# A state-space layer with a mixture layer on one core: one product of each chunk moved from GpSimd to VectorE, and the accumulation of the step sizes moved from a DMA to GpSimd

## The chip, the core and the metric

The kernel runs on one core of a Trainium2 chip. The engines are TensorE (PE), VectorE (DVE), ScalarE (ACT), GpSimd (POOL) and SyncE (SP), which here only issues DMAs. The metric is the device time of one execution in microseconds; smaller is better.

## What is computed

A block of a sequence model on `u` of shape (4, 2048, 256), in float32: a layer norm, a selective state-space layer with residual, a second layer norm, and a mixture of four experts (top 2, with low-rank additions) with residual. The first half, cut to what the change touches:

```python
x, z = jnp.split(u @ W_in.T + b_in, 2, axis=-1)          # 512 channels each
dbc = x @ W_x.T + b_x                                    # 16 + 16 + 16 columns
delta = softplus(dbc[..., :16] @ W_dt.T + b_dt)
def step(h, xs):                                         # over the time steps, h: (B, 512, 16)
    dt_t, x_t, Bt, Ct = xs
    h = h * exp(dt_t[..., None] * A) + x_t[..., None] * (dt_t[..., None] * Bt[:, None, :])
    y_t = einsum('bdn,bn->bd', h, Ct)
    return h, y_t
```

## The kernel before

The input is cut into 16 chunks of 512 time steps, four batches in turn. Partitions hold channels, the free axis holds time. A chunk's recurrence is worked in 16 steps (`s`, lines 1415 and 1486); step `s = 4 m + k` holds channel block `m` (128 channels) and a group `k` of four of the 16 states, spread over 128 partitions as 32 channels x 4 states in four sub-blocks `j`. For each step:

- POOL multiplies the replicated `delta * x` by the replicated B (`times_b`, L1470, 128x2048): the input of the recurrence, in one of four buffers `hs`, one step ahead of the scans. It may only write `hs` when PE has summed the step four before.
- ACT computes the four decays, `exp(dt * a)` (L1203), into four PSUM banks `decay`.
- DVE runs four scans (L1395, 128x512), one for each `j`, with a decay and an input each.
- The states are multiplied by C in two halves of two `j` (128x1024): `h = 0` always on DVE (`times_c` in DVE's part, L1382, from PSUM to `hs`), `h = 1` on POOL for the steps in `POOL_STEPS` and on DVE for the others. For a step of POOL the scans of `j = 2, 3` write to `hs` instead of PSUM, and POOL multiplies in place (L1482). For a step of DVE they write to PSUM, and the product is issued after the first scan of the next step.
- ACT copies the last column to the state of the batch (`keep_state`, L1217), which frees a pair of decay banks for the next step; PE adds the states up (`sum_states`, L998).

`POOL_STEPS` holds the steps with `k < 3`, 12 of 16.

Everything else of the chunk and its neighbours is laid between these steps by hand-written tables, one for each engine (`PE_SIDE`, `ACT_SIDE`, and so on; other tables for the last chunks). A row is a step. "pre" is work for the next chunk, "main" for this one, "post" and "late" for the ones before. The rows that matter here are of POOL (L111): V1 in step 3 and U1 in step 4, for the channel blocks 2 and 3 of this chunk; V0 in step 11 and U0 in step 12, for blocks 0 and 1 of the next; O1 and O2 (Newton steps of the two layer norms, four tiny instructions each) in steps 1 and 7; W0 in step 13. In a step POOL first issues `times_b` of the next step, then `times_c` of the step before, then the side jobs.

V and U make `delta`. The softplus is computed as `relu(v) + log(1 + exp(-|v|))`. ACT leaves `relu(v)` in `z_dt` and the logarithm in `e_dt` (two channel blocks, 128x1024 each). V adds them: a DMA from `z_dt` to `e_dt` that accumulates, issued from POOL (L1460). U waits for it and writes `delta * x` to `z_dt` (L1450, POOL). SP then stores both to HBM (`store_rep`, L755) and reads them back replicated over partitions into `dt_rep` and `dx_rep` (`load_rep`, L722). For the first two channel blocks of the first chunk DVE does both itself (`first_step`, L1398); so there are 31 V and 31 U.

Of the kernel before, what the change touches and what calls it, by code (L numbers as in the profile page):

```python
# [21 lines left out]
ALU = mybir.AluOpType  # L22
# [13 lines left out]
KG = NS // 4  # L36
STEPS = M * KG
# [309 lines left out]
    "",  # L347
]
BANKS = 3
POOL_STEPS = [s for s in range(STEPS) if s % KG < 3]  # L350
V_PAIRS = [(s, h) for s in range(STEPS) for h in range(2) if h == 0 or s not in POOL_STEPS]
BANK_JOBS = "ABCDEFGHIJTK"
LAST_H = 9
# [4 lines left out]
def split_table(table):  # L358
# [17 lines left out]
             pool=[[[x for x in part if x not in ("O1 pre", "V0 pre", "U0 pre")] for part in row] for row in SIDE["pool"]])  # L376
# [111 lines left out]
def block_program(nc, u, w_in, b_in, w_x, b_x, w_dt, b_dt, a_log, d_skip, w_out, b_out, w_ga, b_g, w_i, w_o,  # L488
                  lora_b, ident_in, nsum_in, tri_in, out):
    with ExitStack() as ctx:  # L490
# [3 lines left out]
        def sem(name):  # L494
            return ctx.enter_context(nc.semaphore(name))
# [34 lines left out]
        z_dt = sb("z_dt", [P, 2, T])  # L530
        e_dt = sb("e_dt", [P, 2, T])
# [73 lines left out]
            "xr_loaded", "ln2_part", "ln2_root", "ln2_newton", "x2_ready", "router", "router_exp",  # L605
            "r1_ready", "z2_ready"))
        sp_turn, dve_turn, last_sums = sem("sp_turn"), sem("dve_turn"), sem("last_sums")
        pool_turn, delta_added = sem("pool_turn"), sem("delta_added")
        skip_ready, bound_ready = sem("skip_ready"), sem("bound_ready")
        mask_step, second_step, weight_step = sem("mask_step"), sem("second_step"), sem("weight_step")  # L610
        weights_ready = sem("weights_ready")
# [10 lines left out]
        def pool_products(c, s):  # L622

            return len(POOL_STEPS) * c + POOL_STEPS.index(s) + 1
        out_stored = [sem(f"out_stored{t}") for t in range(TT)]
# [85 lines left out]
        def _(sp):  # L711
# [20 lines left out]
            def waits(*needs):  # L732


                for s_, at in needs:
                    at_least(sp, s_, at)
                    if not isinstance(at, int):
                        sp.sem_inc(sp_turn, 1)
# [9 lines left out]
            def store_rep(c, pair):  # L748


                back = [(loaded[i], 128 * c - (64 if pair == 0 else 0)) for loaded in (dt_loaded, dx_loaded) for i in range(2)]
                waits(*back, (dx_ready, 2 * c + pair + 1))
                for i in (1, 0) if isinstance(c, int) and c == 0 and pair == 0 else range(2):
                    for kind, src in ((1, z_dt), (0, e_dt)):
                        sp.dma_start(rep_dram[kind, 2 * pair + i], src[:, i, :]).then_inc(rep_stored[2 * pair + i], 16)  # L755
# [11 lines left out]
            def body(c, par, parts):  # L767
# [4 lines left out]
                def multiplied(at, s):  # L772

                    if s in POOL_STEPS:
                        return (prod_vector, vector_products(at, s, 0)), (prod_pool, pool_products(at, s))
# [62 lines left out]
        def _(pe):  # L838
# [148 lines left out]
            def sum_states(c, s, odd):  # L987

                m, k = divmod(s, KG)
                if k == 0:  # L990
                    at_least(pe, gated_ready, M * c + m)
                if s in POOL_STEPS:
                    pe.wait_ge(prod_vector, vector_products(c, s, 0))
# [449 lines left out]
        def _(pool):  # L1443

            def job_pool(letter, i, when, job, c, par):
                q, odd = chunk_of(c, when), odd_of(par, when)
                g = nc.gpsimd
                if letter == "U":
                    pool.wait_ge(delta_added, 16 * (2 * q + i))
                    g.tensor_tensor(z_dt[:], e_dt[:], x_t[odd][:, 2 * i:2 * i + 2, :], ALU.mult).then_inc(dx_ready, 1)  # L1450
                elif letter == "O":
                    newton(pool, g, i, q)
                elif letter == "W":
                    pool.wait_ge(second_step, q + 1)
                    g.tensor_tensor(wgt[odd][:, 1], pexp[:, :, NE], wgt[odd][:, 0], ALU.mult).then_inc(weights_ready, 1)
                elif letter == "V":

                    pool.wait_ge(log_dt, 2 * q + i + 1)
                    pool.sem_inc(pool_turn, 1)
                    g.dma_start(e_dt[:], z_dt[:], accum_op=ALU.add).then_inc(delta_added, 16)  # L1460

            def times_b(c, par, s):

# [95 lines left out]
```

## Time and profile before

| | us |
|---|---|
| median of 3 runs | 1874.48 |
| lowest and highest | 1869.98, 1906.22 |
| the profiled execution | 1869.98 |
| its span | 1868.2 |
| mean granted TensorE clock in it | 0.950 |

The span is the time from the first to the last instruction of the profiled execution. The page's first part gives the busy time of each engine, its second the busy share in 40 slices, in which DVE and POOL stand at nine tenths or more from the second slice to the 37th. An engine's busy share is no proof that it paces the others; the waits between engines have to be read beside it. A row of a timeline gives start, duration, engine, line, operation and tiles, and in brackets the idle time before it with what ended it.

### The profile page before, as it was taken

What the parts mean: (1) busy time and instruction counts of PE and PEld (TensorE: products, weight loads), DVE (VectorE), ACT (ScalarE), POOL (GpSimd) and SP (SyncE); (2) the same over time, 40 slices, a digit from 0 to 9 for tenths busy, and PEclk for the clock granted to TensorE, in tenths of its full rate; (3) what the DMA queues carried; (4) which work ended last, traced back from release to release, by engine and by line L of the source; (5) the groups of instructions that cost most, each with busy time, mean ns of one, the idle gap of its engine ahead of it and who ended that gap; (6) DMA issues with size and microseconds to landing.
All of it is one profiled execution on the core that took longest, in us unless ns stands there. A gap on an engine that the chain in (4) does not pass through costs nothing.

```text
span 1868.2 us, 26288 instructions
## 1 busy us (share of the span) xinstructions
PE 1641.5 (88%) x7052; PEld 834.3 (45%) x7052; DVE 1765.0 (94%) x2060; ACT 1505.7 (81%) x3113; POOL 1717.0 (92%) x649
## 2 busy tenths in 40 slices
PE   6646689998998999899899989989998998998999
PEld 3213244444444444444444444444444544444465
DVE  5999999999999999999999999999999999999941
ACT  4776789788888978888897888889788898977743
POOL 1999999999999999999999999999999999999810
PEclk9767889999999999999999999999999999999999
DMA  6565566656647565654756565575656657565100
GB/s 209 137 142 142 109 153 141 163 119 143 151 99 172 132 170 120 148 142 104 174 129 168 126 144 143 105 173 132 163 128 142 144 105 175 120 160 133 42 18 17
DMA packets 150070, 249.07 MB, mean 133 GB/s; under 512 B 22432, under 2 KB 47264, under 8 KB 149408
## 3 DMA queue, kind: packets, MB, share of 16 engines
q1 hardware_dynamic: 145456, 231.09, 51.2%
q0 software_dynamic: 4464, 16.25, 4.5%
q8 instruction: 61, 1.00, 0.2%
q14 instruction: 89, 0.73, 0.1%
HBM read 188.01 MB, written 42.99 MB: 124 GB/s over the span
## 4 chain that ended last, share of the span: by engine, by line
PE 38%; DVE 30%; issue 13%; ACT 8%; POOL 5%; DMA 2%; SPq 1%; DVEq 0%; ACTq 0%; POOLq 0%
DVE decay L1395 13%; DVE hs L1382 8%; PE bank L914 7%; DVE hs L1395 5%; PE y_ps L998 5%; PE bank L962 5%; PE bank L984 4%; PE bank L936 4%; POOL hs L1470 3%; PE bank L918 3%; ACT decay L1203 2%; POOL hs L1482 2%; PE y_ps L1002 2%; PE bank L908 1%; PE bank L979 1%
## 5 line engine op out<-in xcount | busy, mean ns | idle before, releaser
L1470 POOL TENSOR_TENSOR hs<-dx_rep,b_rep 128x2048 f32<-128x2048 f32 x255 | 1180.6, 4643 | 43.6 <-DVE hs L1411 39.7
L1395 DVE TENSOR_TENSOR_SCAN decay<-decay,state,hs 128x512 f32<-128x512 f32 x640 | 798.7, 1288 | 6.3 <-ACT decay L1203 5.2
L1203 ACT ACTIVATE decay<-dt_rep,a_sb 128x512 f32<-128x512 f32 x1024 | 696.2, 686 | 20.6 <-DVE dx_rep L1409 1.8
L1395 DVE TENSOR_TENSOR_SCAN hs<-decay,state,hs 128x512 f32<-128x512 f32 x384 | 491.5, 1280 | 3.9 <-ACT decay L1203 3.8
L1482 POOL TENSOR_TENSOR hs<-hs,c_rep 128x1024 f32<-128x1024 f32 x192 | 469.3, 2444 | 5.3 <-ACT state L1217 4.6
L1382 DVE TENSOR_TENSOR hs<-decay,c_rep 128x1024 f32<-128x1024 f32 x320 | 389.0, 1216 | 0.0
L998 PE MATMUL y_ps<-hs,nsum 128*32 128x512 f32 x2048 | 291.6, 643 | 61.4 <-POOL hs L1482 40.4
L962 PE MATMUL bank<-w_i_sb,x_t 128*128 128x512 f32 x488 | 259.9, 658 | 5.4 <-DVE silu L1282 5.1
L914 PE MATMUL bank<-xn_t,w_in_sb 128*128 128x512 f32 x512 | 249.8, 616 | 12.2 <-DVE silu L1282 4.3
L984 PE MATMUL bank<-w_o_sb,r_t 128*128 128x256 f32 x944 | 221.0, 388 | 10.3 <-ACT r L1181 6.2
L984 PEld LDWEIGHTS bank<-w_o_sb,r_t 128*128 128x128 f32 x944 | 177.6, 192 | 65.0 <-ACT r L1181 18.2
L1217 ACT COPY state<-decay 128x2 f32<-128x2 f32 x320 | 50.4, 157 | 159.8 <-DVE hs L1382 156.7
L914 PEld LDWEIGHTS bank<-xn_t,w_in_sb 128*128 128x128 f32 x512 | 91.7, 194 | 125.7 <-issue 98.3
L979 PE MATMUL bank<-ident,r 128*128 128x128 f32 x928 | 121.7, 277 | 17.2 <-DVE x L1298 14.3
L962 PEld LDWEIGHTS bank<-w_i_sb,x_t 128*128 128x128 f32 x488 | 89.1, 200 | 104.3 <-issue 86.3
L979 PEld LDWEIGHTS bank<-ident,r 128*128 128x128 f32 x928 | 101.8, 140 | 75.6 <-issue 42.7
L998 PEld LDWEIGHTS y_ps<-hs,nsum 128*32 128x32 f32 x2048 | 41.8, 110 | 172.5 <-issue 150.0
L936 PE MATMUL bank<-w_out_sb,gated 128*128 128x256 f32 x480 | 114.0, 380 | 0.1
L1181 ACT ACTIVATE r<-bank,wgt 128x512 f32<-128x512 f32 x122 | 82.3, 675 | 33.0 <-PE bank L885 33.0
L936 PEld LDWEIGHTS bank<-w_out_sb,gated 128*128 128x128 f32 x480 | 91.6, 191 | 13.2 <-DVE gated L1287 0.5
L885 PE MATMUL bank<-lora_st,low_t 64*128 64x512 f32 x122 | 61.0, 500 | 41.1 <-ACT r L1177 40.8
L1177 ACT ACTIVATE r<-bank,wgt 128x512 f32<-128x512 f32 x122 | 82.8, 678 | 15.5 <-PE bank L966 12.2
(182 smaller groups left out, 1853.8 us busy)
## 6 DMA issues: line engine op xcount, KB each, us to landing
dx_rep<-rep_scratch SPq DMA_DIRECT2D x252, 256.0 KB, 4.7
dt_rep<-rep_scratch SPq DMA_DIRECT2D x252, 256.0 KB, 7.6
b_rep<-bc_scratch SPq DMA_DIRECT2D x256, 64.0 KB, 4.0
c_rep<-bc_scratch SPq DMA_DIRECT2D x256, 64.0 KB, 2.4
rep_scratch<-z_dt SPq DMA_DIRECT2D x64, 256.0 KB, 2.6
rep_scratch<-e_dt SPq DMA_DIRECT2D x64, 256.0 KB, 2.8
e_dt<-z_dt POOLq DMA_DIRECT2D x31, 512.0 KB, 4.9
xin<-in_u SPq DMA_DIRECT2D x16, 512.0 KB, 4.0
```

Of the source, the lines that this page charges most:

```text
L914: mm = pe.matmul(ps[:], w_in_sb[:, k, col:col + P], xn_t[odd][:, k, :], start=k == 0, stop=k == KD - 1)
L936: pe.matmul(ps[:, cols], gated[odd][:, k, i * P:(i + 1) * P], w_out_sb[:, k, :], start=k == 0 and is_last(q) and i % 2 == 0, stop=False, s ...
L962: pe.matmul(ps[:], x2_t[odd][:, k, t * P:(t + 1) * P], w_i_sb[:, k, cols], start=k == 0, stop=False, skip_group_check=is_last(q))
L979: mm = pe.matmul(ps[:, f * P:(f + 1) * P], r[i % 2][:, f * P:(f + 1) * P], ident[:], start=r is r1, stop=r is r2, is_transpose=True)
L984: mm = pe.matmul(ps[:, 0:D], r_t[:, f, :], w_o_sb[:, f, :], start=f == 0, stop=f == NF - 1)
L998: mm = pe.matmul(y_ps[32 * j:32 * j + 32, :], nsum[:], hs[s % 4][:, j, :], start=k == 0, stop=k == KG - 1, skip_group_check=True)
L1177: nc.scalar.activation(r1[i % 2][:], ps[:], ACT.Relu, scale=wgt[odd][:, 0, i // 2:i // 2 + 1]).then_inc(r1_ready, 1)
L1203: nc.scalar.activation(decay[:, j, :], dt_rep[m % 2][:, j, :], ACT.Exp, scale=a_sb[:, J * s + j:J * s + j + 1]).then_inc(decay_ready, 1)
L1382: v.tensor_tensor(hs[s % 4][:, js, :], decay[:, js, :], c_rep[:, k, :].unsqueeze(1).to_broadcast([P, 2, T]), ALU.mult).then_inc(prod_vecto ...
L1395: v.tensor_tensor_scan(hs[s % 4][:, j, :] if kept else decay[:, j, :], decay[:, j, :], hs[s % 4][:, j, :], state[:, b, n:n + 1], ALU.mult, ...
L1470: nc.gpsimd.tensor_tensor(hs[s % 4][:], dx_rep[m % 2][:], b_rep[:, k, :].unsqueeze(1).to_broadcast([P, J, T]), ALU.mult).then_inc(input_re ...
L1482: nc.gpsimd.tensor_tensor(hs[s % 4][:, 2:4, :], hs[s % 4][:, 2:4, :], c_rep[:, k, :].unsqueeze(1).to_broadcast([P, 2, T]), ALU.mult).then_ ...
```

## The change

Two edits that belong together.

1. V becomes a POOL instruction: `e_dt = e_dt + z_dt`, 128x1024, on POOL. It signals on `delta_ready`, which the first step on DVE used already; U waits for that, and so does `store_rep` on SP, beside its old wait for `dx_ready`. Two semaphores and the `sem_inc` ahead of the DMA go. V's and U's places in the tables stay.
2. `POOL_STEPS` loses step 14 (`m = 3, k = 2`). The second half of its product with C goes to DVE, between the first and the second scan of step 15; its scans of `j = 2, 3` write to PSUM. PE then waits for DVE's product alone in that step, ACT copies that state from PSUM, and all counts of products follow from the lists.

```diff
-POOL_STEPS = [s for s in range(STEPS) if s % KG < 3]
+POOL_STEPS = [s for s in range(STEPS) if s % KG < 3 and s != 14]
@@
-        pool_turn, delta_added = sem("pool_turn"), sem("delta_added")
@@ store_rep
-                waits(*back, (dx_ready, 2 * c + pair + 1))
+                waits(*back, (delta_ready, 2 * c + pair + 1), (dx_ready, 2 * c + pair + 1))
@@ job_pool
                 if letter == "U":
-                    pool.wait_ge(delta_added, 16 * (2 * q + i))
+                    pool.wait_ge(delta_ready, 2 * q + i + 1)
@@
                 elif letter == "V":
 
                     pool.wait_ge(log_dt, 2 * q + i + 1)
-                    pool.sem_inc(pool_turn, 1)
-                    g.dma_start(e_dt[:], z_dt[:], accum_op=ALU.add).then_inc(delta_added, 16)
+                    g.tensor_tensor(e_dt[:], e_dt[:], z_dt[:], ALU.add).then_inc(delta_ready, 1)
```

## Rows read from the trace of the kernel before

**Rows 1.** The page's first part: busy time, share of the span, instructions, by engine.
```profile
PE 1641.5 (88%) x7052; PEld 834.3 (45%) x7052; DVE 1765.0 (94%) x2060; ACT 1505.7 (81%) x3113; POOL 1717.0 (92%) x649
```

**Rows 2.** Busy time in a steady stretch, and DVE's once-a-chunk wait, first and last.
```profile
403.80:1606.70 1202.90, 1102.06 (x4812) 565.21 (x4811) 1194.65 (x1378) 1034.14 (x2150) 1188.93 (x453) 0.98 0.60 141
...
420.84 1.28 DVE L1395 TENSOR_TENSOR_SCAN hs<-decay,state,hs 128x512 f32<-128x512 f32 x1 [0.21 <-ACT decay L1203]
...
1513.59 1.28 DVE L1395 TENSOR_TENSOR_SCAN hs<-decay,state,hs 128x512 f32<-128x512 f32 x1 [0.21 <-ACT decay L1203]
```

**Rows 3.** Waits of DVE and POOL in that stretch: us in total, times, longest.
```profile
DVE lg L1325 <- PE bank L946: 4.9, 6, 0.9
POOL z_dt L1450 <- DMA e_dt<-z_dt: 4.4, 10, 0.9
DVE hs L1395 <- ACT decay L1203: 2.5, 11, 0.4
POOL hs L1470 <- PE y_ps L998: 1.7, 5, 1.0
POOL hs L1482 <- ACT state L1217: 0.9, 4, 0.2
DVE decay L1395 <- issue: 0.8, 1, 0.8
```

**Rows 4.** Timeline of DVE, steps 15 and 0 of two chunks.
```profile
685.46 3.64 DVE L1395 TENSOR_TENSOR_SCAN decay<-decay,state,hs 128x512 f32<-128x512 f32 x3
...
692.47 1.23 DVE L1382 TENSOR_TENSOR hs<-decay,c_rep 128x1024 f32<-128x1024 f32 x1
693.59 1.30 DVE L1395 TENSOR_TENSOR_SCAN decay<-decay,state,hs 128x512 f32<-128x512 f32 x1
694.78 1.28 DVE L1395 TENSOR_TENSOR_SCAN hs<-decay,state,hs 128x512 f32<-128x512 f32 x1
```

**Rows 5.** Timeline of POOL around V0 and U0, and a later U1.
```profile
660.61 2.38 POOL L1482 TENSOR_TENSOR hs<-hs,c_rep 128x1024 f32<-128x1024 f32 x1
662.91 0.83 POOL L1460 DMA_DIRECT2D e_dt<-z_dt  x1
663.52 4.80 POOL L1470 TENSOR_TENSOR hs<-dx_rep,b_rep 128x2048 f32<-128x2048 f32 x1
668.03 2.60 POOL L1450 TENSOR_TENSOR z_dt<-e_dt,x_t 128x1024 f32<-128x1024 f32 x1
670.35 4.78 POOL L1470 TENSOR_TENSOR hs<-dx_rep,b_rep 128x2048 f32<-128x2048 f32 x1
...
722.82 2.38 POOL L1450 TENSOR_TENSOR z_dt<-e_dt,x_t 128x1024 f32<-128x1024 f32 x1 [0.41 <-DMA e_dt<-z_dt]
```

**Rows 6.** Timeline of ACT at the same place as rows 4.
```profile
693.73 0.16 ACT L1217 COPY state<-decay 128x2 f32<-128x2 f32 x1 [0.44 <-DVE hs L1382]
693.92 0.69 ACT L1203 ACTIVATE decay<-dt_rep,a_sb 128x512 f32<-128x512 f32 x1
```

**Rows 7.** Timelines of POOL (inputs of steps 9, 10) and DVE (steps 9 and 13).
```profile
637.98 9.04 POOL L1470 TENSOR_TENSOR hs<-dx_rep,b_rep 128x2048 f32<-128x2048 f32 x2
646.97 2.37 POOL L1482 TENSOR_TENSOR hs<-hs,c_rep 128x1024 f32<-128x1024 f32 x1
...
643.67 2.44 DVE L1395 TENSOR_TENSOR_SCAN decay<-decay,state,hs 128x512 f32<-128x512 f32 x2
...
672.13 2.48 DVE L1395 TENSOR_TENSOR_SCAN decay<-decay,state,hs 128x512 f32<-128x512 f32 x2
```

**Rows 8.** Timeline of PE: the sum of step 8.
```profile
651.15 1.06 PE L998 MATMUL y_ps<-hs,nsum 128*32 128x512 f32 x8
```

**Rows 9.** Timelines of POOL and DVE where the second chunk begins.
```profile
140.00 5.03 POOL L1470 TENSOR_TENSOR hs<-dx_rep,b_rep 128x2048 f32<-128x2048 f32 x1
...
143.74 2.61 DVE L1395 TENSOR_TENSOR_SCAN decay<-decay,state,hs 128x512 f32<-128x512 f32 x2
```

**Rows 10.** The page's DMA issues: KB each, median us to landing.
```profile
dx_rep<-rep_scratch SPq DMA_DIRECT2D x252, 256.0 KB, 4.7
...
e_dt<-z_dt POOLq DMA_DIRECT2D x31, 512.0 KB, 4.9
```

**Rows 11.** Timelines of SP and POOL: the reload after U1, and its first use.
```profile
728.16 1.77 SPq L722 DMA_DIRECT2D dx_rep<-rep_scratch  x4
...
738.78 4.53 POOL L1470 TENSOR_TENSOR hs<-dx_rep,b_rep 128x2048 f32<-128x2048 f32 x1
```

## Prediction

> **What bounds the kernel now.** The page's first part comes first [rows 1]: DVE is busy for 94% of the span and POOL for 92%, PE for 88%, ACT for 81%. Two engines are close to full, so the average does not say which one paces. I then asked for the busy times of the steady stretch, eleven chunks long [rows 2]: DVE 1194.65 of 1202.90 us, POOL 1188.93. The start and the length of a chunk come from a DVE wait that returns once in each (eleven of them, first and last shown): (1513.59 - 420.84) / 10 = 109.3 us a chunk [rows 2].
>
> Next the list of waits of that stretch [rows 3]. DVE waits for PE (the router's input, 4.9 us in 11 chunks) and for ACT's decays (2.5 us), and never for POOL's inputs `hs`; with one issue gap of 0.8 that is 8.2 us, 0.75 a chunk. POOL waits for PE (1.7), for ACT (0.9) and for its own accumulating DMA (4.4 us, 10 times). So the chunk is DVE's own instruction stream, about 108.5 us, plus 0.75 of waits; POOL has a queue of inputs ahead of it and is held only by those who free its buffers. The prediction is therefore a sum over DVE, plus a check of whether POOL, made slower, overtakes it from behind.
>
> **The product of step 14 moves to DVE.** Each of the 16 chunks gives DVE one more 128x1024 product. Its reported duration is about 1.22 us, but the next instruction starts 1.12 us later (692.47 to 693.59) [rows 4], and on a full engine the spacing counts: 16 x 1.12 = 17.9 us (19.5 by durations, 1.22). Nothing hides it, since DVE does not idle at that place: from 685.46 on the scans of step 15 follow one another, three in 3.64 us [rows 4]. POOL loses one product of 2.30 us (660.61 to 662.91) [rows 5] per chunk.
>
> Step 14 then behaves as steps 3, 7, 11 and 15 do: the scans j = 2, 3 stay in PSUM, and ACT may only refill decay banks 2 and 3 for step 15 once DVE's product is over. After step 15's own second product (692.47, over at 693.69) ACT copies the state at 693.73 and starts the decay at 693.92; it is done at 694.61, and the scan that needs it starts at 694.78 [rows 4, 6]. The margin is 0.17 us, and at one of the four such places in a chunk, in step 8, it is already missed by 0.2 (the DVE wait in [rows 2]). Step 8 has two ACT side jobs between the second decay and that copy, step 15 has none there. I take 0 and keep 0.2 x 16 = 3 us for the range. PE's sum of step 14 now waits for DVE alone, which it trails by more than a step (it takes step 8 at 651.15, when DVE, at step 9 from 643.67, is in step 10) [rows 7, 8]; no change.
>
> **The accumulation moves from a DMA to a POOL add.** There are 31. The add is not in the trace; its nearest row is POOL's product of the same shape on the same tiles, L1450: 668.03 to 670.35, 2.32 us [rows 5]. The DMA issue that goes away takes 0.61 us by starts (662.91 to 663.52) and 0.83 by its reported duration. The following POOL instruction is reported as 4.80 us, though two of its kind usually take 9.0 [rows 7]: something of POOL stays about 0.25 us behind after an issue. So the exchange costs POOL 1.7 us by starts (2.32 - 0.61) and 1.5 by completion (2.32 - 0.61 - 0.25). I take 1.7. Against it, U no longer waits for the landing (4.4 us in 22, 0.41 at 722.82) [rows 3, 5].
>
> The Trainium skill ("Perfetto Trace Analysis", GPSIMD Engine Instruction) says that a GpSimd instruction's reported span is unreliable and should be timed by start-to-start spacing. By that rule an exchange is 1.7 us and the 31 of them 53 us of POOL; by the reported spans (2.38 at 722.82 less 0.83) it would be 1.55 and 48 us. The trace agrees as far as the starts of the next instructions do not move with the longer spans.
>
> Per chunk POOL's work changes by 2 x 1.7 - 2.3 = +1.1 us, DVE's by +1.12. On average they keep step. What matters is where in the chunk POOL is short.
>
> The tightest place is steps 7 to 9, after V1 and U1 and the Newton steps O2. The input of step 9 starts at 637.98, half of 9.04 us later it is ready, at 642.5, and DVE's scan of step 9 starts at 643.67: 1.1 us ahead [rows 7]. V1 takes 1.7 from this. The DMA wait before a U gives back 0.4 (4.4 us in 10 of 22) [rows 3]. The product that POOL no longer does at the end of the chunk lets it start steps 0 to 3 a little earlier, but only as far as PE has freed the buffers; I set 0.3 for that, a judgement, bounded by 0 and by the 1.12 by which DVE itself comes later. 1.1 - 1.7 + 0.4 + 0.3 = 0.1 us: just not late on average, late by a few tenths in some chunks. I book a wait of 0.1 us in 14 chunks, 1.4 us in all. POOL's product of step 8 ends at 649.34 and PE takes it at 651.15 [rows 8]; a POOL 1 us later still finds PE not waiting.
>
> V0's add falls in steps 11 to 12, where POOL is 3.8 us ahead (663.52 + 4.80 = 668.3; DVE's scan of that step starts at 672.13) [rows 5, 7], so it is covered there in a steady chunk. In the first chunk it is not: there POOL starts with nothing ahead and reaches step 0 of the second chunk just in time, 140.00 + 5.03 = 145.03, and DVE's second scan of the pair at 143.74 (1.31 each) starts at about 145.06 [rows 9]. Two exchanges (3.4, less 0.5 of lag that vanishes) against DVE's own 1.1: DVE waits 1.8 us there, once: POOL's step 14 product came after that input and does not help it, but from there on it adds 2.3 us of lead.
>
> **The loads behind it.** U ends 1.3 to 1.7 us later, so `store_rep` on SP and the two `load_rep` behind it do too; the added SP wait is met whenever the old one is. POOL itself needs the loaded `dx_rep`, and it is late by the same amount: issued from 728.16, landed 4.7 us after an issue, by about 735, used at 738.78 [rows 10, 11]. The margin of nearly 4 us stands. The DMA traffic that vanishes (31 transfers of 512 KB) was waited for only by U. I book 0.
>
> **Sum.** 17.9 + 1.4 + 1.8 = 21.1 us on the profiled execution's 1870.0 us (span 1868.2): 1891. The median of the runs shown is 4.5 above that execution; I add half of it and say 1893.
>
> **Rivals.**
>
> *POOL overtakes DVE* (slower). If the relief at steps 7 to 9 does not come, because POOL's start at steps 0 to 3 is set by PE's sums and these move with DVE, DVE waits 1.7 - 1.1 = 0.6 us in each chunk: 14 x 0.6 = 8 us, 1899. If PE in turn falls behind the late POOL product and gives buffers back late, the whole 1.7 is lost: 14 x 1.7 = 24 us, 1870 + 18 + 2 + 24 = 1914, over 2%. For it: 4.9 of DVE's 8.2 us of waits hang on PE already [rows 3]. Against it: PE takes POOL's product 1.8 us after its end [rows 8]. It decides from 1.2 us of waiting a chunk on.
>
> *DVE's idle takes the product* (not slower). If PE's schedule and not DVE's stream sets the chunk, the 0.75 us of DVE waits are slack that the new product fills: 17.9 - 16 x 0.75 = 6 us, 1876, no measurable change. Against it: the wait for PE comes in only 6 of 11 chunks, and it is at step 10, far from step 15.
>
> *The DMA held POOL back* (faster). The POOL instruction after each issue is reported 0.25 us longer. If that were real slowness, and for some ten instructions after each of 31 issues, 31 x 10 x 0.25 = 78 us of POOL would come back; less the 18 of the net exchange (16 x 1.1) that is 60, and with POOL as the bound the time would be 1870 - 60 = 1810. Against it: their starts still follow at 4.5 and 2.3 us [rows 5], and DVE, with 8 us of idle in 1203, could not go faster anyway. The Trainium skill ("SBUF — State Buffer", Who interferes with whom) says that DMAs never contend with compute engines, except that a DMA issued from GpSimd can be starved of descriptor writing by some DVE instructions; by that rule too something could come back. The trace agrees only in small: U's waits for the landing are 4.4 us in all.
>
> **Chances.** Forecast (DVE pays, POOL just holds), 0.6; POOL overtakes mildly, to 1908, 0.2; over 2%, 0.08; DVE's idle takes it 0.1; faster 0.02. The range takes in 1876 of the third and the mild second with the 3 us of ACT: 1876 to 1910; the likeliest case's own is 1885 to 1899. Two per cent is about what this measurement tells from no change: faster 0.02, within 0.9, slower 0.08.
>
> **What would show it.** L1382 counts 336, L1482 176, 31 adds of V with a spacing of 2.3 us. A chunk of 110.4 to 110.6 us. In the list of waits, DVE waits for POOL's `hs` L1470: a few tenths at steps 7 to 9, one of 1.5 to 2 us near 145 us. If that wait is absent, the lead was larger than I read; if it is over 1 us a chunk, POOL is the pacer. If the chunk stays at 109.3, DVE was not the bound.

## The result, and the profile after

The kernel after takes 1899.38 us (median of 4 runs, 1898.83 to 1904.81) against 1875.7 us of the kernel before on the same chip (1869.98 to 1906.22). The ratio is 1.0153, with an interval of 1.013 to 1.0178: slower, by less than 2%. (A ratio is an estimate of its own and not the quotient of the two medians, which is 1.0126; executions over 1.5% above the fastest of their kernel, here that of 1906.22 us, are left out of it.) The profiled execution took 1897.28 us, its span is 1895.3 us and its granted TensorE clock 0.938; that of before had a span of 1868.2 us at a clock of 0.950. The spans differ by 27.1 us, the medians by 23.7, the forecast's own difference was 21 to 23.

The page of after: the engines' busy time (answers [rows 1]), the clock row of its 40 slices, and four groups of instructions (count | busy us, mean ns | idle before them).

```profile
PE 1670.8 (88%) x7052; PEld 849.0 (45%) x7052; DVE 1784.0 (94%) x2076; ACT 1504.9 (79%) x3113; POOL 1725.3 (91%) x633
...
PEclk9768789998999999999999988999999889999999
...
L1468 POOL TENSOR_TENSOR hs<-dx_rep,b_rep 128x2048 f32<-128x2048 f32 x255 | 1158.4, 4552 | 55.7 <-DVE hs L1410 40.1
L1480 POOL TENSOR_TENSOR hs<-hs,c_rep 128x1024 f32<-128x1024 f32 x176 | 417.7, 2373 | 11.9 <-ACT state L1216 7.5
L1381 DVE TENSOR_TENSOR hs<-decay,c_rep 128x1024 f32<-128x1024 f32 x336 | 402.8, 1199 | 0.0
L997 PE MATMUL y_ps<-hs,nsum 128*32 128x512 f32 x2048 | 295.8, 651 | 64.7 <-POOL hs L1480 46.9
```

(The line numbers of after are one lower than those of before on PE, ACT and DVE, two lower on POOL: the scan L1395 is now L1394, DVE's product L1381, the decay L1202, the router's read L1324, POOL's input L1468 and its product L1480.) DVE is busy 19.0 us longer, POOL only 8.3 us. The products have moved: 336 on DVE, 176 on POOL. In the clock row the first six slices are the start. Behind them it falls below nine tenths in slices 10, 24, 25, 32 and 33 of 47.4 us each, that is near 450, 1140 and 1520 us.

DVE's waits of nearly the whole span, from 50 us to 1790 us (us in total, times, longest), first before, then after.

```profile
DVE lg L1325 <- PE bank L946: 6.0, 8, 0.9
DVE decay L1395 <- ACT decay L1203: 5.2, 8, 1.4
DVE hs L1395 <- ACT decay L1203: 3.8, 15, 0.5
```

```profile
DVE decay L1394 <- ACT decay L1202: 9.3, 8, 1.7
DVE lg L1324 <- PE bank L945: 8.6, 7, 2.1
DVE hs L1394 <- ACT decay L1202: 5.5, 14, 0.8
DVE decay L1394 <- POOL hs L1468: 2.6, 7, 0.7
```

That gives the ledger of the two executions. DVE's added product is 16 x 1.12 = 17.9 us. Waits for ACT's decays rise from 9.0 to 14.8 us (+5.8), for PE at the router from 6.0 to 8.6 (+2.6), and waits for POOL, which did not exist, are 2.6. The sum is 28.9 us, and 0.8 us of an issue gap of before [rows 3] is gone: 28.1, against 27.1 measured. The first and the last item of the ledger were in the forecast. The 8.4 us between them were not, and most of the experiments are about these.

By chunks, measured from the first scan of a chunk to that of the next: the quiet ones took 108.6 us before and 109.75 after, which is the product and no more (in each of them step 15 grew from 5.83 to 6.97 us). But three chunks of after took 113.45, 113.69 and 114.13. Before had none over 110.57.

Such long chunks, DVE's timeline in steps 10 and 11 of the first and the last: two waits, the same pair in each of the three.

```profile
443.54 0.17 DVE L1324 TENSOR_TENSOR lg<-bank,b_g_sb 128x16 f32<-128x16 f32 x1 [1.45 <-PE bank L945]
...
449.16 1.29 DVE L1394 TENSOR_TENSOR_SCAN decay<-decay,state,hs 128x512 f32<-128x512 f32 x1 [1.67 <-ACT decay L1202]
...
1554.42 0.17 DVE L1324 TENSOR_TENSOR lg<-bank,b_g_sb 128x16 f32<-128x16 f32 x1 [2.14 <-PE bank L945]
...
1560.04 1.29 DVE L1394 TENSOR_TENSOR_SCAN decay<-decay,state,hs 128x512 f32<-128x512 f32 x1 [1.67 <-ACT decay L1202]
```

PE's timeline ahead of the first of these waits, and the same instructions in a quiet chunk further on; then one ACT instruction between the two waits.

```profile
436.50 0.66 PE L907 MATMUL bank<-ident,xr 128*128 128x128 f32 x4 [1.54 <-ACT e_dt L1100]
437.84 0.66 PE L907 MATMUL bank<-ident,xr 128*128 128x128 f32 x4 [0.68 <-ACT x_t L1162]
438.42 1.54 PE L997 MATMUL y_ps<-hs,nsum 128*32 128x512 f32 x8
439.89 3.60 PE L945 MATMUL bank<-w_ga_sb,x_t 128*128 128x20 f32 x16
443.33 3.76 PE L961 MATMUL bank<-w_i_sb,x_t 128*128 128x512 f32 x4
...
660.75 0.66 PE L907 MATMUL bank<-ident,xr 128*128 128x128 f32 x4 [1.54 <-ACT e_dt L1100]
662.08 0.66 PE L907 MATMUL bank<-ident,xr 128*128 128x128 f32 x4 [0.68 <-ACT x_t L1162]
662.67 1.07 PE L997 MATMUL y_ps<-hs,nsum 128*32 128x512 f32 x8
664.02 1.96 PE L945 MATMUL bank<-w_ga_sb,x_t 128*128 128x20 f32 x16 [0.29 <-ACT x_t L1162]
665.83 1.96 PE L961 MATMUL bank<-w_i_sb,x_t 128*128 128x512 f32 x4
```

```profile
447.85 0.69 ACT L1176 ACTIVATE r<-bank,wgt 128x512 f32<-128x512 f32 x1 [3.74 <-PE bank L965]
```

The same two stretches in sum (busy us of PE, PE's loads, DVE, ACT, POOL, then the granted clock, DMA share, GB/s), and behind them the fourth chunk of the kernel before at the same place.

```profile
438.00:448.00 10.00, 10.00 (x34) 5.54 (x34) 8.04 (x15) 6.13 (x13) 10.00 (x3) 0.54 0.59 114
...
656.00:666.00 10.00, 7.49 (x53) 4.27 (x52) 10.00 (x10) 9.90 (x21) 10.00 (x3) 1.00 0.88 186
```

```profile
431.00:441.00 10.00, 9.14 (x37) 4.46 (x37) 9.13 (x17) 8.76 (x18) 10.00 (x3) 0.83 0.62 125
```

From 438 to 448 us the granted clock is 0.54, the lower of its two levels (1.2 of 2.4 GHz) for most of the stretch. The router's sixteen matmuls take 3.60 us where they take 1.96, and the four that follow 3.76. The router's output is late for DVE (1.45 us). ACT stands for 3.74 us before it reads `bank` in L1176; its decay for step 11 is behind that in its own order, and DVE waits 1.67 us for it. Before the fall PE had idled 1.54 and 0.68 us, but in the quiet chunk it idled just so (660.75 and 662.08) and kept the full clock. The Trainium skill ("TensorE: Matmul & The Clock Gate", HAM oscillation) says that the gate passes one of two rates and can fall again in the middle of a kernel when PE idles between bursts. The trace agrees with the two rates (1.96 and 3.60 us for the same sixteen) and leaves open what decides between two chunks with the same idle.

The clock fell at this place in the kernel before too, only for less of the stretch: 0.83 in its fourth chunk, where DVE waits 0.87 us at the router and not at all for the decay of step 11. What sets the long chunks apart is how much of this place runs at the lower level. Taken from 68 to 79 us behind a chunk's first scan, the granted clock is 0.53 to 0.57 in the long chunks of after, and 0.84 or 1.00 in its others from the third on.

DVE's seven waits for POOL all came in three chunks, the first, the second and the tenth; two of them:

```profile
134.69 1.29 DVE L1394 TENSOR_TENSOR_SCAN decay<-decay,state,hs 128x512 f32<-128x512 f32 x1 [0.26 <-POOL hs L1468]
...
1082.62 3.64 DVE L1394 TENSOR_TENSOR_SCAN decay<-decay,state,hs 128x512 f32<-128x512 f32 x3 [0.68 <-POOL hs L1468]
```

And POOL at V0's add of a steady chunk, where [rows 5] showed the DMA:

```profile
673.10 2.38 POOL L1480 TENSOR_TENSOR hs<-hs,c_rep 128x1024 f32<-128x1024 f32 x1
675.41 2.38 POOL L1458 TENSOR_TENSOR e_dt<-e_dt,z_dt 128x1024 f32<-128x1024 f32 x1
677.73 4.57 POOL L1468 TENSOR_TENSOR hs<-dx_rep,b_rep 128x2048 f32<-128x2048 f32 x1
```

The add takes 2.32 us by starts, as the row of the product of that shape had said. The input behind it is reported with 4.57 us instead of 4.80.

### The profile page after: what moved, and what is told of

It is laid out like the page before. It is cut to its first block, busy times and chain, and to the rows that moved or that the text cites. A ratio compares the mean times of both kernels' runs of the same rounds, so it can differ in the third digit from the quotient of the medians.

```text
span 1895.3 us, 26178 instructions
## 1 busy us (share of the span) xinstructions
PE 1670.8 (88%) x7052; PEld 849.0 (45%) x7052; DVE 1784.0 (94%) x2076; ACT 1504.9 (79%) x3113; POOL 1725.3 (91%) x633
## 4 chain that ended last, share of the span: by engine, by line
DVE 35%; PE 24%; issue 18%; POOL 15%; ACT 4%; DVEq 0%; ACTq 0%; POOLq 0%
DVE decay L1394 15%; DVE hs L1381 10%; POOL hs L1468 9%; DVE hs L1394 6%; POOL hs L1480 4%; PE bank L913 4%; PE y_ps L997 3%; PE bank L961 3%; PE bank L983 3%; PE bank L935 2%; ACT decay L1202 1%; PE bank L917 1%; PE bank L978 1%; POOL e_dt L1458 1%; DVE gated L1286 1%
## 5 line engine op out<-in xcount | busy, mean ns | idle before, releaser
L1468 POOL TENSOR_TENSOR hs<-dx_rep,b_rep 128x2048 f32<-128x2048 f32 x255 | 1158.4, 4552 | 55.7 <-DVE hs L1410 40.1
L1394 DVE TENSOR_TENSOR_SCAN decay<-decay,state,hs 128x512 f32<-128x512 f32 x672 | 830.7, 1269 | 12.5 <-ACT decay L1202 9.8
L1202 ACT ACTIVATE decay<-dt_rep,a_sb 128x512 f32<-128x512 f32 x1024 | 696.2, 686 | 20.6 <-DVE dx_rep L1408 1.8
L1394 DVE TENSOR_TENSOR_SCAN hs<-decay,state,hs 128x512 f32<-128x512 f32 x352 | 445.0, 1264 | 5.7 <-ACT decay L1202 5.5
L1480 POOL TENSOR_TENSOR hs<-hs,c_rep 128x1024 f32<-128x1024 f32 x176 | 417.7, 2373 | 11.9 <-ACT state L1216 7.5
L1381 DVE TENSOR_TENSOR hs<-decay,c_rep 128x1024 f32<-128x1024 f32 x336 | 402.8, 1199 | 0.0
L997 PE MATMUL y_ps<-hs,nsum 128*32 128x512 f32 x2048 | 295.8, 651 | 64.7 <-POOL hs L1480 46.9
L961 PE MATMUL bank<-w_i_sb,x_t 128*128 128x512 f32 x488 | 270.1, 681 | 5.7 <-DVE silu L1281 4.7
L913 PE MATMUL bank<-xn_t,w_in_sb 128*128 128x512 f32 x512 | 252.2, 622 | 11.8 <-DVE silu L1281 4.3
L961 PEld LDWEIGHTS bank<-w_i_sb,x_t 128*128 128x128 f32 x488 | 93.2, 210 | 110.8 <-issue 93.7
L978 PE MATMUL bank<-ident,r 128*128 128x128 f32 x928 | 126.4, 281 | 18.1 <-DVE x L1297 13.8
L978 PEld LDWEIGHTS bank<-ident,r 128*128 128x128 f32 x928 | 103.5, 142 | 78.9 <-issue 39.8
L1176 ACT ACTIVATE r<-bank,wgt 128x512 f32<-128x512 f32 x122 | 82.5, 676 | 19.3 <-PE bank L965 15.5
```

The costliest lines, as they stand in the source:

```text
L913: mm = pe.matmul(ps[:], w_in_sb[:, k, col:col + P], xn_t[odd][:, k, :], start=k == 0, stop=k == KD - 1)
L961: pe.matmul(ps[:], x2_t[odd][:, k, t * P:(t + 1) * P], w_i_sb[:, k, cols], start=k == 0, stop=False, skip_group_check=is_last(q))
L978: mm = pe.matmul(ps[:, f * P:(f + 1) * P], r[i % 2][:, f * P:(f + 1) * P], ident[:], start=r is r1, stop=r is r2, is_transpose=True)
L997: mm = pe.matmul(y_ps[32 * j:32 * j + 32, :], nsum[:], hs[s % 4][:, j, :], start=k == 0, stop=k == KG - 1, skip_group_check=True)
L1176: nc.scalar.activation(r1[i % 2][:], ps[:], ACT.Relu, scale=wgt[odd][:, 0, i // 2:i // 2 + 1]).then_inc(r1_ready, 1)
L1202: nc.scalar.activation(decay[:, j, :], dt_rep[m % 2][:, j, :], ACT.Exp, scale=a_sb[:, J * s + j:J * s + j + 1]).then_inc(decay_ready, 1)
```

## The experiments

Every ratio is to the kernel before, timed on the same chip in the same session. The theory at the start: DVE pays for its product, POOL for its adds, and the place of each decides who waits. The rivals: POOL overtakes DVE; the excess over 18 us comes from elsewhere.

### The add alone

The kernel after, with all products of POOL in place.

```diff
-POOL_STEPS = [s for s in range(STEPS) if s % KG < 3 and s != 14]
+POOL_STEPS = [s for s in range(STEPS) if s % KG < 3]
```

> The second edit is undone: V is the POOL add, but POOL keeps the product of step 14. Theory (each engine pays by its own stream, DVE sets the pace while POOL's inputs come in time): POOL now has 2 x 1.7 = 3.4 us more a chunk than in the kernel before, where it had about 1.3 us to spare, so POOL takes over: a chunk of 111.3 to 112, 1903 to 1915 us, and DVE waits for POOL's inputs (L1468 to L1470) in every chunk, 2 to 3 us. Rival (the time of the changed kernel is DVE's added product and POOL hardly matters): 1875 to 1885 us.

Measured: 1911.53 us (1909.93 to 1917.94), ratio 1.0169 (1.0108 to 1.0231), so that it is open whether it is over 2%. DVE's waits from 50 to 1790 us:

```profile
DVE decay L1394 <- ACT decay L1202: 29.8, 41, 2.9
DVE hs L1394 <- ACT decay L1202: 8.5, 25, 1.4
DVE decay L1394 <- POOL hs L1468: 7.0, 14, 1.8
DVE lg L1324 <- PE bank L945: 4.2, 4, 2.1
```

The time is where a POOL that overtakes would have it, yet DVE waits for POOL itself only 7 us. 38 us are waits for ACT's decays. What holds ACT is in its own list of waits, over the same stretch:

```profile
ACT xin L1158 <- POOL nt L691: 28.4, 14, 3.7
```

`nt` is the result of POOL's Newton steps, `xin` that of the norm on ACT. The Newton steps stand behind POOL's inputs and adds in its order; the norm on ACT waits for them, and the decays stand behind the norm on ACT. So a late POOL reaches DVE first by way of its small side work and ACT's order, not by its big tile. After shows two such waits only, 3.3 us. The half of the change that moves a product from POOL to DVE is what makes the other half bearable: the add alone is slower than both together.

### Step 14 alone

The kernel before, with the second edit only.

```diff
-POOL_STEPS = [s for s in range(STEPS) if s % KG < 3]
+POOL_STEPS = [s for s in range(STEPS) if s % KG < 3 and s != 14]
```

> The first edit is undone: the accumulation stays a DMA, only the product of step 14 is on DVE. Theory: 16 x 1.12 = 18 us over the kernel before and nothing else, 1888 to 1891 us, no wait of DVE for POOL. If the 6 to 9 us that the changed kernel has beyond that come from POOL's lateness, they are gone here. Rival (they come from TensorE's half-clock stretches at the router, which a longer chunk shifts in time, whatever POOL does): they stay, 1895 to 1900 us, with a mean clock of 0.94.

Measured: 1897.65 us (1889.6 to 1902.29, 10 runs), ratio 1.008 (1.0043 to 1.0117). The profiled execution, 1895.75 us at a clock of 0.938, has quiet chunks of 109.76 us, and among the others again some of 113.4 to 114.1. Its waits:

```profile
DVE decay L1395 <- ACT decay L1203: 10.3, 8, 1.7
DVE lg L1325 <- PE bank L946: 9.0, 7, 2.1
DVE hs L1395 <- ACT decay L1203: 5.6, 14, 1.1
...
DVE decay L1395 <- POOL hs L1470: 0.2, 1, 0.2
```

The waits for the router and for decays are those of after, with the DMA in place and POOL relieved of 16 x 2.3 = 37 us of products. The excess is therefore not POOL's. What the add costs on top is POOL's 2.6 us and little else.

### Another step for the product

The kernel after, with step 6 in place of step 14: the product is taken from POOL right ahead of the tight steps 7 to 9.

```diff
-POOL_STEPS = [s for s in range(STEPS) if s % KG < 3 and s != 14]
+POOL_STEPS = [s for s in range(STEPS) if s % KG < 3 and s != 6]
```

> As the changed kernel, but it is step 6 whose second product goes to DVE, ahead of the place (steps 7 to 9) where POOL's lead is smallest, and not step 14. Theory: POOL is 2.3 us further ahead at steps 7 to 9, so the waits of DVE for POOL there (2.7 us in all) go; but the total is DVE's stream again, 1890 to 1900. Rival (it is the place of the product that costs, since ACT's decays come late after it): 3 us or more above the changed kernel, with more waits of DVE for ACT's decays.

Measured: 1907.11 us (1902.85 to 1911.77), ratio 1.0136 (1.0074 to 1.0199), at a clock of 0.945. DVE's wait for POOL falls to 0.6 us, as meant, and its waits for decays rise:

```profile
DVE decay L1394 <- ACT decay L1202: 21.6, 43, 1.6
DVE hs L1394 <- ACT decay L1202: 3.7, 15, 0.5
```

ACT now waits 24.2 us for `nt` (14 times). POOL is relieved at step 6 and late at steps 0 to 3, where the Newton steps for the next norm stand. Step 14 relieves it just before them.

### That norm later

The same kernel, with the norm's jobs on ACT, which read `nt`, moved two places on.

```diff
-    " |  | R1 pre | S2 late, J3 late, O0 pre, O1 pre",
-    "O2 pre, O3 pre |  | T2 late | S3 late, A0 pre",
+    " |  | R1 pre | S2 late, J3 late",
+    "O0 pre, O1 pre | O2 pre, O3 pre | T2 late | S3 late, A0 pre",
```

> As e3_step6_instead, and ACT applies the first layer norm (O0 to O3) one part of a step later. In e3 ACT waited there 14 us in all for POOL's Newton steps, which are late as POOL still has the product of step 14 ahead of them; ACT works in order, so the decays of steps 2 and 3 came late and DVE waited 0.5 us a chunk and more. Theory: this wait goes, with DVE's waits for decays at steps 2 and 3, and the time falls by 5 to 10 us to 1898 to 1903. Rival (the decays are late for another reason, PE's sums): no change, 1905 to 1909.

Measured: 1906.3 us (1904.64 to 1908.78), ratio 1.0103 (1.0031 to 1.0174). ACT's wait for `nt` is gone and comes back one link on: PE waits for the norm (8.8 us between 400 and 1600 us), ACT for PE, DVE for ACT. Timelines of ACT and DVE at one such place:

```profile
613.72 0.38 ACT L1070 ACTIVATE x<-bank 128x256 f32<-128x256 f32 x1 [1.56 <-PE bank L939]
...
614.80 1.29 DVE L1394 TENSOR_TENSOR_SCAN decay<-decay,state,hs 128x512 f32<-128x512 f32 x1 [1.19 <-ACT decay L1202]
```

No gain shows. My reading is that the chain has no room at any of its links there. But the two executions differ in the router's waits as well (4.6 us here, 0.5 in that of the last experiment), so that a gain of a few microseconds could be hidden.

### Fill PE ahead of the router

The kernel after, with three more 128x256 matmuls ahead of the transposes G0 of each chunk. They write to the bank that the transposes overwrite, and add nothing to the output.

```diff
+                    if letter == "G" and i == 0 and not is_last(q):
+                        for f in range(3):
+                            pe.matmul(ps[:, 0:D], ident[:], w_o_sb[:, f, :], start=True, stop=True, skip_group_check=True)
                     pe.wait_ge(xn_ready if letter == "A" else x2_ready, TT * (q + 1))
```

> The changed kernel, with three matmuls of 128x256 more in each chunk, on PE ahead of the transposes G0, where PE waits 1.5 us for ACT; their result is overwritten. Theory: the late router input (H0) and the late decay of step 11 come from matmuls at half clock just behind that idle time; with PE busy there the stretches of half clock at step 10 go, and with them most of DVE's 8.6 us of waits for PE and 5 us of waits for ACT at step 11: 1888 to 1893 us. Rival (the clock falls with the total work and not with that idle time): same as the changed kernel, 1897 to 1901, or slower if the filler delays PE.

Measured: 1901.85 us (1899.64 to 1904.1), ratio 1.011 (1.0052 to 1.0169); clock 0.951. The filler starts only when its bank is free, after the idle time and not in it, so that it puts off the transposes and, through ACT, a decay:

```profile
770.30 1.56 PE L906 MATMUL bank<-w_o_sb,ident 128*128 128x256 f32 x6 [1.54 <-ACT e_dt L1103]
...
773.54 1.29 DVE L1397 TENSOR_TENSOR_SCAN decay<-decay,state,hs 128x512 f32<-128x512 f32 x1 [1.12 <-ACT decay L1205]
```

Such waits come in nearly each chunk, 19.6 us in 19 times, where after had 9.3 in 8. Against that the router's waits fall from 8.6 us to 0.5, no chunk is over 112.3 us, and the clock stands at 0.951 against 0.938. The balance of the two spans is +2.3 us, and the median is about that of the 21 executions of after on record (1901.5): what the low clock costs this kernel is about what the filler costs.

### Read the router's output later

The kernel after, with DVE's reads of it one scan later.

```diff
-    " |  | H0 post | H1 post, S2 main, H2 post",
+    " |  |  | H0 post, S2 main, H1 post, H2 post",
```

> The changed kernel; DVE reads the router's product (H0) one scan later, in the fourth part of step 10 and not the third, in all chunks but the last two. Theory: DVE's waits for PE there (0.9 to 2.1 us, in 5 of 11 chunks) shrink by 1.2 us each, so all but the longest go: 4 to 5 us, 1894 to 1896. Rival (ACT is late at that place as well, for the same matmuls): DVE waits for ACT's decay at step 11 by as much, no gain.

Measured: 1902.44 us (1894.38 to 1908.66, 10 runs), ratio 1.0101 (1.0061 to 1.0142). The waits for the router shrink to 2.0 us, and those for the decay of step 11 grow from 1.67 to 2.70 us in the two long chunks:

```profile
780.14 1.29 DVE L1394 TENSOR_TENSOR_SCAN decay<-decay,state,hs 128x512 f32<-128x512 f32 x1 [2.70 <-ACT decay L1202]
```

A wait that DVE misses at step 10 it meets at step 11, since ACT is held by the same slow matmuls. The place of the read is not the cause.

### Two products moved

The kernel before, with the products of steps 13 and 14 on DVE.

```diff
-POOL_STEPS = [s for s in range(STEPS) if s % KG < 3]
+POOL_STEPS = [s for s in range(STEPS) if s % KG < 3 and s not in (13, 14)]
```

> The kernel before (the accumulation is a DMA), with the second products of both steps 13 and 14 on DVE. Theory (DVE sets the pace, each product is paid by its spacing): twice the 18 us of one product, 36 us over the kernel before at the same clock, a quiet chunk of 108.6 + 2 x 1.12 = 110.9 us. Rival (DVE's waits of 0.75 us a chunk are slack and fill up): less than 30 us, and fewer DVE waits.

Measured: 1921.06 us (1918.89 to 1924.7), ratio 1.019 (1.0118 to 1.0263), so that here too 2% lies inside the interval. The quiet chunk is 110.91 us, 2.3 more than before: a product costs DVE 1.15 us, twice over. Four others take 115.0 to 115.1 us, each with the pair of waits, and the clock is 0.919 to 0.924 in all runs. The sum of DVE's stream was right; the rest is waits, 29.0 us against the 16.6 of the first profile of before.

### The kernel before again

It was run a second and a third time, nothing changed but a comment, to see its own spread.

> The kernel before, unchanged. Theory (TensorE's clock explains how executions of one kernel differ, by late router matmuls at step 10 of a chunk): an execution with a granted clock below 0.945 shows chunks of 112 to 114 us among those of 108.6 and 109.6, with DVE waits for the router's input of more than 1 us and for a decay of 1.7 us right after, just as the changed kernel. Rival (these long chunks are the changed kernel's own): none of them in the kernel before at any clock.

Measured: 1877.38 us (1869.97 to 1903.77, 10 runs), ratio 0.9992 (0.9953 to 1.0031). The profiled execution, 1876.22 us, has a steady chunk of 109.19 us, and from the third chunk on none over 110.2. (Its second took 112.51 us, where that of the first profile took 109.32, and its first scan starts 2.9 us later: that is the whole difference between the two.) Its clock was 0.946, so that it did not answer what an execution at a low clock looks like. The third time did:

> The kernel before, unchanged, for a profile of an execution with a lower clock. Theory: if it falls below 0.94, chunks of 112 to 114 us show, with the router read late at step 10 and a decay late at step 11. If it is near 0.95, it shows nothing new.

Measured: one run of 1887.33 us at a clock of 0.938, that of after's profile. Its chunks include three of 112.76, 112.77 and 112.95 us, and in each DVE shows the pair of waits that after shows:

```profile
882.02 0.17 DVE L1325 TENSOR_TENSOR lg<-bank,b_g_sb 128x16 f32<-128x16 f32 x1 [1.86 <-PE bank L946]
...
887.64 1.29 DVE L1395 TENSOR_TENSOR_SCAN decay<-decay,state,hs 128x512 f32<-128x512 f32 x1 [1.67 <-ACT decay L1203]
```

So the long chunk is not the change's own. Its place is the same, and so is the clock there: 0.53 to 0.54 from 68 to 79 us behind the first scan, as in the long chunks of after. (The four of step 14 alone have 0.53 to 0.56, the four of two products 0.53 to 0.56.) The profile of before with which the forecast worked, at 0.950, was simply one of the kernel's best executions.

### Step 6 with the DMA

The kernel before, with the product of step 6 on DVE.

```diff
-POOL_STEPS = [s for s in range(STEPS) if s % KG < 3]
+POOL_STEPS = [s for s in range(STEPS) if s % KG < 3 and s != 6]
```

> The accumulation is a DMA as before, and the product of step 6 (not 14) is on DVE; so it stands to e2_step14_alone as e3_step6_instead stands to the changed kernel. Theory (the place of the product matters only because the POOL adds make POOL late where the chunk begins, and its Newton steps hold up ACT's norm, PE's transposes and through ACT's order the decays): POOL has 3.4 us a chunk more room here, so the place costs little: 1894 to 1899 us, as e2, with at most a few waits of ACT for POOL's Newton steps. Rival (DVE or ACT have less room at step 6 than at step 14 whatever POOL does): 5 us or more above e2, as e3 is above the changed kernel.

Measured: 1886.75 us (1883.4 to 1895.62, 10 runs), ratio 1.0016 (0.9975 to 1.0057): below what was expected, and 11 us below step 14 alone. The clock is 0.942 to 0.951, its median 0.947, where step 14 alone has 0.9385; the profiled execution waits 3.3 us at the router, in three places. A product costs DVE the same in either step (quiet chunk 109.54 here, 109.76 there, and here DVE's wait of 0.21 us at step 8 is gone), but with it in step 6 the router's matmuls keep the full clock more often. Why they do, I did not settle.

### One filler in the kernel before

The filler above, one matmul in place of three, in the kernel before.

```diff
+                        for f in range(1):
+                            pe.matmul(ps[:, 0:D], ident[:], w_o_sb[:, f, :], start=True, stop=True, skip_group_check=True)
```

> The kernel before with one extra matmul of 128x256 a chunk ahead of the transposes G0. In e4, three of them were not hidden (PE waited for the bank to be freed, not for the data, so they ran behind the idle time and delayed G0 by 1.3 us), yet the granted clock was 0.951 and not 0.937. Theory: one costs 0.45 us a chunk, 7 us, and gives the clock back in part: 1875 to 1882 us with a clock of 0.945 to 0.95 in all executions, so a narrower spread than the kernel before has. Rival (the clock in e4 was chance): 0.935 to 0.95 as before, and the time 5 to 7 us above the kernel before.

Measured: 1877.6 us (1872.81 to 1879.21, 10 runs), ratio 0.9972 (0.9938 to 1.0007). All ten had a clock of 0.946 to 0.952; the kernel before, in the same session, went from 1871.14 to 1899.11 us at 0.928 to 0.950 (19 runs). The quiet chunk is 108.99 us, 0.38 longer. The filler, which the trace has as two instructions:

```profile
653.35 0.70 PE L907 MATMUL bank<-w_o_sb,ident 128*128 128x256 f32 x2 [1.54 <-ACT e_dt L1104]
```

It too comes behind the idle time and not in it. So with one short matmul in each chunk no execution at a low clock came, at about the price that these have on average; by what way it keeps the clock, the runs do not show. It is the best version of the study, but by less than can be measured.

## Why the forecast was right, and where it was not

It said 1893 us within 1876 to 1910, and same within 2%; 1899.38 lies in the range and the ratio 1.0153 under the 2%. Point by point:

- **The product on DVE.** Right, and the whole of it: 1.12 us by starts was booked, quiet chunks grew by 1.14, all of it in step 15. Nothing hid it, and two products cost twice that. Counts were as listed (336, 176, 31 adds at 2.32 us by starts). Taking the spacing of the starts and not the reported 1.22 us (19.5 us) was right.
- **ACT's margin at step 15.** It held: the quiet chunk grew by 1.14 us, of which 1.12 is the product, so the 0.2 a chunk kept in the range did not come.
- **POOL at steps 7 to 9.** The forecast let the lead there fall by 1.0, to 0.1 us. Over the chunks the lead of the input over the scan fell at steps 7, 8 and 9 from 1.60, 1.26 and 1.12 us to 0.75, 0.45 and 0.42, with 0.12 at the lowest: it fell by 0.15 to 0.3 us less than booked. The term at fault is U's wait for the DMA, which I had put at 0.4 us a chunk by its listed idle time. By starts it was worth 0.7: U1 came 5.20 us behind the start of the input ahead of it (median of eleven chunks) where 4.50 is usual, and after has 4.50. The listed idle is short because the input ahead, the first behind the DMA issue, is reported too long. For the 0.3 that I had set for step 14 by judgement nothing speaks: at step 4, before V1 can act, the lead is 3.5 us before and after, and step 14 alone, which has the relief and not the adds, has 1.30, 0.97 and 0.91. Waits for POOL were 1.3 us in the steady stretch and 2.6 in all, 3.2 were booked. The input and U1 behind it in one chunk, first before (5.27 us apart by starts), then after (4.49):

```profile
608.93 4.78 POOL L1470 TENSOR_TENSOR hs<-dx_rep,b_rep 128x2048 f32<-128x2048 f32 x1
614.20 2.38 POOL L1450 TENSOR_TENSOR z_dt<-e_dt,x_t 128x1024 f32<-128x1024 f32 x1 [0.49 <-DMA e_dt<-z_dt]
```

```profile
622.14 4.57 POOL L1468 TENSOR_TENSOR hs<-dx_rep,b_rep 128x2048 f32<-128x2048 f32 x1
626.63 2.41 POOL L1449 TENSOR_TENSOR z_dt<-e_dt,x_t 128x1024 f32<-128x1024 f32 x1
```

- **The wait near 145 us.** Wrong in its form: no single one of 1.8 us, but two, of 0.26 and 0.18, before it. The first chunk took 3.0 us longer than before, of which 1.2 are the product and 1.2 a wait for a decay at 127.92 us. That wait is in the add alone too and not in step 14 alone, whose first chunk took 2.0 us less than that of after; so the adds cost there about the 1.8 us that were booked, but mostly by way of ACT, and the sum had gone by POOL alone: its size was luck.
- **The rival "POOL overtakes"** had the right size for a kernel without the second edit (1911.53 measured, 1914 in its upper form), by luck, and the wrong road: not the inputs, but Newton steps, ACT's norm and ACT's decays. The check of leads looked only at the big tiles. It happened to be enough, since step 14 relieves POOL ahead of that small work; with step 6 it would have promised a gain and missed 6 to 8 us.
- **The rival "DVE's idle takes the product"** is out: DVE's waits grew. **"The DMA held POOL back"** is out too. Its premise was that the 0.25 us in the reported durations was real; without the DMA the durations shrink (4.57 us for 4.80) and the starts follow at the same 4.5 and 2.3 us. The Trainium skill ("Perfetto Trace Analysis", GPSIMD Engine Instruction) says to time such instructions by their starts; the trace agrees, with 677.73 - 675.41 = 2.32 us where [rows 5] has 2.32 for a product that was itself reported with 2.60.
- **The loads** cost nothing, as booked: DVE, POOL and PE have no new wait for a DMA.

**The step that fell short is the last, the base of the sum.** It put 21.1 us on an execution of 1870 us and added half of the gap to the median, 2.3 us, for all else; DVE's waits for PE and ACT were taken over as they stood. A ledger of all thirteen profiled executions shows what they do. The last column is the span less all DVE waits of its list (50 to 1790 us), which is DVE's own stream with the two ends:

| kernel | clock | span | DVE waits for ACT, PE, POOL | waits, sum | rest |
|---|---|---|---|---|---|
| before | 0.950 | 1868.2 | 9.0, 6.8, 0 (0.8 of issue) | 16.6 | 1851.6 |
| before, again | 0.946 | 1874.3 | 12.1, 7.7, 0 | 19.8 | 1854.5 |
| before, third | 0.938 | 1885.4 | 18.3, 14.6, 0 | 32.9 | 1852.5 |
| before, one filler | 0.949 | 1875.7 | 16.6, 6.2, 0 | 22.8 | 1852.9 |
| step 6, DMA | 0.946 | 1884.8 | 11.4, 4.1, 0 | 15.5 | 1869.3 |
| step 14, DMA | 0.938 | 1893.6 | 15.9, 9.8, 0.2 | 25.9 | 1867.7 |
| after | 0.938 | 1895.3 | 14.8, 9.3, 2.6 | 26.7 | 1868.6 |
| after, read later | 0.940 | 1891.6 | 16.0, 2.0, 3.2 | 21.2 | 1870.4 |
| after, three fillers | 0.951 | 1897.6 | 25.4, 0.5, 1.8 (0.7 of issue) | 28.4 | 1869.2 |
| step 6, add | 0.945 | 1903.5 | 25.3, 1.3, 0.6 | 27.2 | 1876.3 |
| step 6, add, norm later | 0.939 | 1905.8 | 23.6, 5.3, 1.8 | 30.7 | 1875.1 |
| add alone | 0.946 | 1908.1 | 38.3, 4.5, 7.0 | 49.8 | 1858.3 |
| two products, DMA | 0.924 | 1916.6 | 17.2, 11.8, 0 | 29.0 | 1887.6 |

With no product moved the rest is 1852 to 1854.5, with one 1868 to 1870, with two 1888: 16 to 17.5 us for each by the means, near the 17.9 of the forecast. Part of the spread is the start, which the rest contains: the first scan comes at 39.8, 42.7, 41.6 and 41.5 us in the first four lines and at 39.7 to 40.2 us in the next five and the last. With this time taken off as well the rest is 1810.9 to 1811.8 for none, 1828.0 to 1830.4 for one and 1847.5 for two, that is 17.7 and 18.0 us for each. (In the three lines where POOL is late through the norm, step 6 with the add in both forms and the add alone, some 6 us more are in no listed wait. Most of them are in DVE's busy time: 1771.8 us in the add alone, where before has 1765.0 for the same 2060 instructions. A product is reported with 1.22 us and its successor starts after 1.12; before a wait this overlap is lost. The add alone has 85 listed waits, before 33: by my estimate 52 x 0.1 = 5 us.)

All else is waits. The kernel before has 16.6 us of them in one execution and 32.9 in another, 16 us apart (the spans 17) with not one instruction changed, and the first was the execution that I took as the base. It was the fastest of the three runs shown. Of the 27.1 us between the two profiles, 17 are the product, 2.6 are POOL, and 7.5 are those waits.

Over 52 executions of the kernel before, a line through time and mean clock falls by 14 us for each 0.01 of the clock, with 2.9 us of scatter around it. I had read the router's waits (4.9 us in 11 chunks) and the clock of 0.950, and not asked what those waits become at another clock. A base for the sum would have been the median, with its whole gap of 4.5 us: 1896. Over all executions on record the median of before is 1879.8 us (52) and that of after 1901.5 (21), 21.8 us apart where the sum said 21.1. So the size of the change was right, to a microsecond, and its base, 1870 us and the 2.3 added, was 7.5 us low. Some of that agreement is luck, since the change in clock and waits that comes with it was in no term.

**What stays open.** The median clock is 0.942 for before (52 executions) and 0.937 for after (21); 0.9385 for step 14 with the DMA, 0.947 for step 6 with it (10 each), 0.92 with two products moved (4). The place of DVE's product goes with how often PE's clock falls; by what way, no run shows. PE idles before the router both where the clock falls and where it doesn't. Nor is it settled how much of the 24 us between the medians is the change's own by way of the clock, and how much is chance: at a clock of 0.938 the third profile of before is only 10 us faster than that of after, since at that clock before waits more. At a clock of 0.938 or 0.939 the median is 1886.0 us for before (five of the 52 executions) and 1899.0 for after (three of the 21), 13 us apart.

## What to carry to other kernels

Where one engine's stream is the chunk, an instruction added to it costs its spacing of starts, to a few hundredths of a microsecond, and moving work to it is worth only what the relieved engine was holding back. When a nearly full engine gets more work, follow its small side work too, through every engine that takes it in order: its large tiles had a lead, its Newton steps had none. And before a difference of one per cent is put down to an edit, take the waits of the bounding engine out of both spans and compare what is left; the waits are to be compared over several executions of the old kernel.

## What the runs showed of the hardware

- The same program, on one core, took 1870 to 1899 us in nearly all of its executions, at a mean granted TensorE clock of 0.950 down to 0.928 (the highest of all, 1906.22). TensorE is not the busiest engine (88%); the loss comes where a stretch at the lower clock (1.2 of 2.4 GHz) meets a place without slack, here up to 4 us in a chunk.
- A stretch at the lower clock makes the sixteen 128x20 matmuls of the router 3.60 us instead of 1.96 and doubles four 128x512 ones (3.76 for 1.96).
- One more 128x256 matmul (and what goes with it, 0.70 us of PE) ahead of that place kept the clock at 0.946 to 0.952 in ten of ten runs, and the spread at 6 us against 28. Three kept it at 0.946 to 0.951 in four of four, and cost a wait of 1.1 us in nearly each chunk.
- 31 DMAs of 512 KB that add into SBUF, gone from the DMA queues, changed nothing on POOL's starts beyond their issue and the wait for them: inputs follow at 4.5 us with and without.
